# Block-quantised feed-forward weights: nine parts of half size per matrix, one in each projection chunk, and the block scales from a scalar and two tensors

## The chip, the cores and the metric

One core of a Trainium2 chip runs the whole program. The metric is device time in microseconds (us), the median of several executions; lower is better. The engines are TensorE (PE, with PEld for its weight loads), VectorE (DVE), ScalarE (ACT), GpSimd (POOL) and SyncE (SP), which issues the DMAs. Each engine runs its own instructions in the order in which they were written, and waits on semaphores for the others.

## What is computed

The kernel is one pre-norm transformer block over X of shape (8, 2048, 256) in float32:

```
x = x + attention(layernorm(x))     Q = xpos(x Wq), K = xpos(x Wk), V = x Wv
                                    (softmax(Q K^T) * 0.9^|n-m|) V
x = x + ffn(layernorm(x))           down(silu(gate(x)) * up(x)), 704 hidden features

quantised(v), for every block of 16 values along a row, before each linear layer of ffn:
    scale = max(max|v| / 6, 1e-12)
    v / scale rounded to the nearest of 0, .5, 1, 1.5, 2, 3, 4, 6 with its sign, times scale
```

The three feed-forward weights (gate, up, down) are quantised like the activations. Each is held as 128 partitions x 1408 values, so 88 blocks of 16 in a partition.

## The kernel before, in words

**Two stages.** The first stage goes over the input in 32 chunks of 512 rows (batch by batch, four chunks each; the last four chunks are batch 0, which stays on the chip). A chunk is normalised, transposed on TensorE, multiplied with Wk, Wq and Wv, rotated (xpos) and written to DRAM. The second stage goes over 128 row tiles: scores, softmax, decay, values and the feed-forward layers. The change touches the first stage alone.

**A chunk on each engine.** PE does in this order the keys (12 matmuls of 512 columns, tile score), the transposes of the next chunk (L492, 8), queries (12 more) and values (24 of 256). VectorE does, for chunk c: the statistics of chunk c+2 (L1039 to L1047), the rotation of the keys (L1061 to L1063, tile rot_k), the lower half of the next chunk's transposed input (L1052, tile xT), the rotation of the queries (L1061 to L1063, tile rot_q), and then one part of the weights, if any. In the last four chunks it also keeps the values on the chip (L1078, vals) before that part. POOL does: the reciprocal standard deviation of chunk c+2 (L859, rstd), the sum of the rotated keys (L863, rot_k), the sum of the rotated queries (L869, q_stage), the lower half of the keys (L874, keys), and then its own part of the weights, if any. ScalarE normalises chunk c+2 in place (L693, L697, x_in) once rstd is there, and PE transposes that in the middle of the chunk after.

**The weights.** They are quantised in the shade of the first stage by `weights(u)` on VectorE and on POOL, called at the end of each chunk u with `n, part = divmod(u - W_FROM, W_CHUNKS)`: n is the matrix (gate, up, down). With W_CHUNKS = 10, VectorE does for matrix n in chunks 2 + 10n to 7 + 10n: block maxima (L1089), scales and their reciprocals (L1011, L1013), the division by the scales (L1093), the exponent (L1016), the rounding grid (L1019) and the rounding (L1023), each over the whole matrix. POOL does in chunks 8 + 10n to 11 + 10n the subtraction of the grid (L884), in two halves, and the multiplication by the scales (L887), in two halves. The sources and results are slices of buffers that the second stage uses later: gate_in, hq_buf and down_in for the matrices, h_buf for the grid, xv, xe and xq for maxima and scales. SP loads matrix n in chunk n * W_CHUNKS (L379).

A part of VectorE starts when the rotation of the queries is done, at which moment POOL's sum of the queries (L869) has its data as well. The lines that set this:

```
for i in range(B):
    for c in range(NC):
        chunk(i, c)
        weights(i * NC + c)
```

Of the kernel before, what the change touches and what calls it, by code (L numbers as in the profile page):

```python
# [11 lines left out]
ALU = mybir.AluOpType  # L12
# [3 lines left out]
P = 128  # L16
# [31 lines left out]
WARM = (30, 12)  # L48
W_FROM, W_CHUNKS = 2, 10
V_SPLIT = (10, 12, 14, 0, 1, 3, 5, 7)  # L50
# [73 lines left out]
def build(nc, X, WQ, WK, WV, WG, WU, WD, rot_tab, decay_tab, eye, out):  # L124
# [5 lines left out]
    with ExitStack() as ctx:  # L130
# [34 lines left out]
        st2, mv2, var2, rstd2, rstd6 = sb("st2", [P, 6]), sb("mv2", [P, 2]), sb("var2", [P, 1]), sb("rstd2", [P, 1]), sb("rstd6", [P, 1])  # L165
        aggr_pad = sb("aggr_pad", [P, 1])
        minus_half, six, minus_rstd = sb("minus_half", [P, CT]), sb("six", [P, 1]), sb("minus_rstd", [P, CT])
        smax, nmax = sb("smax", [P, 2]), sb("nmax", [P, 2])
# [72 lines left out]
        hq_step, hv_ready, hg_ready, hq_ready = sem("hq_step"), sem("hv_ready"), sem("hg_ready"), sem("hq_ready")  # L241
        NSTEP_W, NSTEP_LN2, NSTEP_XQ, NSTEP_HQ = 6, 2, 6, 5

# [42 lines left out]
        def blocks(ap):  # L286
            return ap.rearrange("p (b k) -> p b k", k=QB)
# [562 lines left out]
        def _(pool):  # L850
# [26 lines left out]
            def weights(u):  # L877

                n, part = divmod(u - W_FROM, W_CHUNKS)
                h, part = part % 2, part // 2  # L880
                half, few = slice(h * WC // 2, (h + 1) * WC // 2), slice(h * WB // 2, (h + 1) * WB // 2)
                if 0 <= n < 3 and part == 3:
                    pool.wait_ge(w_rounded, n + 1)
                    pool.tensor_tensor(w_stage[n][:, half], w_stage[n][:, half], w_exp[:, half], ALU.subtract).then_inc(w_levelled, 1)  # L884
                if 0 <= n < 3 and part == 4:
                    pool.wait_ge(w_levelled, 2 * n + h + 1)
                    pool.tensor_tensor(blocks(w_stage[n][:, half]), blocks(w_stage[n][:, half]), spread(ws[n][:, few], WB // 2), ALU.mult).then_inc(w_quant, 1)  # L887
# [107 lines left out]
        def _(dve):  # L995
# [13 lines left out]
            def scales(then, wait, am, s, rs):  # L1009

                then(dve.tensor_scalar(s, am, SIXTH, 1e-12, ALU.mult, ALU.max))  # L1011
                wait()
                then(dve.reciprocal(rs, s))  # L1013
# [66 lines left out]
            def weights(u):  # L1080

                n, part = divmod(u - W_FROM, W_CHUNKS)
                if not 0 <= n < 3 or part > 5:
                    return
                then, wait, count = chain(w_step, n * NSTEP_W + (0, 1, 3, 4, 5, 6)[part])
                wait()
                if part == 0:
                    dve.wait_ge(w_loaded[n], 16)
                    then(dve.tensor_reduce(wam, blocks(w_stage[n]), AX.X, ALU.max, apply_absolute_value=True))  # L1089
                elif part == 1:  # L1090
                    scales(then, wait, wam, ws[n], wrs)
                elif part == 2:
                    then(dve.tensor_tensor(blocks(w_stage[n]), blocks(w_stage[n]), spread(wrs, WB), ALU.mult))  # L1093
                elif part == 3:
                    if n:
                        dve.wait_ge(w_levelled, 2 * n)
                    exponent(then, w_stage[n], w_exp)
                elif part == 4:
                    grid(then, w_exp)
                else:  # L1100
                    rounded(w_stage[n], w_exp, w_rounded)

# [10 lines left out]
            for x in mv1:  # L1113
                dve.memset(x[:, :, 2], EPS).then_inc(eps_set, 1)
            dve.wait_ge(eps_set, 2)
            def projection_weights(order):
# [236 lines left out]
```

## Time and profile before

| what | us |
|---|---|
| median of 3 runs | 2570.81 (2567.68 to 2571.44) |
| the profiled execution, its own time | 2572.08 |
| its span in the profile | 2570.3 |
| PE busy | 2535.4 (99%) |
| VectorE busy | 2148.3 (84%) |
| POOL busy | 1819.8 (71%) |
| ScalarE busy | 1505.4 (59%) |

The granted TensorE clock is 0.997 of full speed over the span. The profile's page gives busy times and groups; its timeline gives single instructions with start, length, engine, line, operation, output and inputs, and in square brackets the idle time of that engine just before and who ended it. The first stage ends at about 319 us, where the first score of the second stage starts. An instruction's length in the timeline includes the time that it stands on its engine without being able to work.

### The profile page before, as it was taken

The page shows a single profiled execution, that of the slowest core. Times are in us where ns is not written, and L with a number is a line of the kernel's source. Part 1 is how long each engine was busy: PE and PEld are TensorE (multiplying, and loading weights), DVE is VectorE, ACT ScalarE, POOL GpSimd, SP SyncE. Part 2 cuts the span into 40 slices and gives each one's busy share as a digit, 9 for nine tenths or more (in the row PEclk, how much of TensorE's full clock was granted, in tenths as well). Part 3 has the DMA queues.
Part 4 walks back from the last instruction along what each step waited for, and adds up shares of the span by engine and source line. Part 5 has one row for each costly group of instructions (what it writes and reads, how often), then busy time and mean ns, then how long its engine had stood idle before and what let it go on. Part 6 is the DMA issues. An engine that isn't in the chain of part 4 may idle for free.

```text
span 2570.3 us, 51983 instructions
## 1 busy us (share of the span) xinstructions
PE 2535.4 (99%) x16188; PEld 2293.8 (89%) x16188; DVE 2148.3 (84%) x4784; ACT 1505.4 (59%) x2966; POOL 1819.8 (71%) x1919
## 2 busy tenths in 40 slices
PE   9999989999999999999999999999999999999998
PEld 8888879999999999989999899989999999989997
DVE  8999868888888888788888888888888888888886
ACT  5666555566656655656555665566566656565654
POOL 6999947667766767667766766667766776667665
PEclk9999999999999999999999999999999999999999
DMA  8777510113111311131111311131113111221110
GB/s 286 278 282 283 192 55 23 44 34 109 40 46 30 110 42 46 32 106 44 34 42 53 98 32 46 36 108 38 46 32 106 44 42 34 78 74 40 38 38 22
DMA packets 163474, 203.29 MB, mean 79 GB/s; under 512 B 15184, under 2 KB 116752, under 8 KB 163216
## 3 DMA queue, kind: packets, MB, share of 16 engines
q1 hardware_dynamic: 163216, 200.01, 24.0%
q8 instruction: 142, 2.33, 0.4%
q14 instruction: 116, 0.95, 0.1%
HBM read 103.42 MB, written 77.59 MB: 70 GB/s over the span
## 4 chain that ended last, share of the span: by engine, by line
PE 81%; DMA 1%; issue 1%; SPq 1%; DVE 1%; POOL 1%; ACT 1%; DVEq 0%; ACTq 0%; POOLq 0%
PE score L483 26%; PE acc L615 19%; PE ring L483 18%; PE acc L483 8%; PE ring L583 6%; PE ring L635 3%; DMA keys<-k_dram 1%; PE ring L574 1%; PE acc L657 1%; SPq L414 1%; ACT probs L783 0%; POOL h_buf L962 0%; POOL h_buf L956 0%; POOL hq_buf L969 0%; DVE h_buf L1250 0%
## 5 line engine op out<-in xcount | busy, mean ns | idle before, releaser
L483 PE MATMUL score<-keys,q_st 128*128 128x512 f32 x3072 | 761.3, 396 | 7.1 <-ACT probs L783 3.4
L483 PEld LDWEIGHTS score<-keys,q_st 128*128 128x128 f32 x3072 | 559.6, 189 | 117.3 <-issue 3.8
L615 PE MATMUL acc<-vals,pT 128*128 128x256 f32 x3984 | 557.1, 287 | 0.8 <-DVE pT L1154 0.8
L941 POOL TENSOR_TENSOR probs<-probs,decay 128x512 f32<-128x512 f32 (+3 forms) x416 | 446.9, 1087 | 144.4 <-ACT probs L783 144.4
L483 PE MATMUL ring<-w_gu,xqT 128*128 128x512 f32 (+1 forms) x2304 | 509.1, 374 | 0.0
L615 PEld LDWEIGHTS acc<-vals,pT 128*128 128x128 f32 x3984 | 499.2, 189 | 6.1 <-DVE pT L1154 2.0
L483 PEld LDWEIGHTS ring<-w_gu,xqT 128*128 128x128 f32 x2304 | 418.6, 188 | 63.2
L753 ACT ACTIVATE pT<-ring 128x512 fp32r<-128x512 f32 (+3 forms) x432 | 226.9, 535 | 380.2 <-PE ring L583 372.7
L1167 DVE TENSOR_REDUCE smax<-score 128x1 f32<-128x1024 f32 x256 | 312.4, 1220 | 105.7 <-PE score L483 104.8
L1154 DVE TENSOR_TENSOR pT<-ring,pT 128x512 fp32r<-128x512 f32 (+3 forms) x432 | 251.0, 606 | 69.0 <-ACT pT L753 67.9
L947 POOL TENSOR_TENSOR xv<-xv,xe 128x256 f32<-128x256 f32 x128 | 94.4, 738 | 274.0 <-DVE xv L1023 274.0
L753 ACT ACTIVATE xqT<-ring 128x256 fp32r<-128x256 f32 x128 | 49.2, 385 | 401.5 <-PE ring L574 401.5
L783 ACT ACTIVATE probs<-score,nmax 128x1024 f32<-128x1024 f32 x256 | 282.8, 1116 | 0.1
L483 PE MATMUL acc<-w_dn,hT 128*128 128x256 f32 x1920 | 239.3, 277 | 4.6 <-DVE hT L1154 4.6
L483 PEld LDWEIGHTS acc<-w_dn,hT 128*128 128x128 f32 x1920 | 236.0, 188 | 5.3 <-DVE hT L1154 5.3
L936 POOL TENSOR_TENSOR edge_probs<-probs,decay 128x128 f32<-128x128 f32 x144 | 69.0, 479 | 228.8 <-ACT probs L783 228.8
L962 POOL TENSOR_TENSOR h_buf<-h_buf 128x704 f32<-128x704 f32 x128 | 218.8, 1709 | 4.3 <-DVE h_buf L1023 4.3
L1250 DVE TENSOR_TENSOR h_buf<-h_buf,ring 128x256 f32<-128x256 f32 (+1 forms) x384 | 144.2, 376 | 75.7 <-ACT h_buf L809 75.4
L753 ACT ACTIVATE hT<-ring 128x512 fp32r<-128x512 f32 (+1 forms) x256 | 125.0, 490 | 124.9 <-PE ring L635 124.9
L1154 DVE TENSOR_TENSOR hT<-ring,hT 128x512 fp32r<-128x512 f32 (+1 forms) x256 | 141.4, 554 | 66.4 <-ACT hT L753 66.4
L583 PE MATMUL ring<-ident,probs 128*128 128x128 f32 x1328 | 195.2, 273 | 0.0
L483 PE MATMUL score<-xT,w_in 128*128 128x512 f32 x768 | 188.9, 395 | 5.8 <-DVE xT L1052 5.8
(132 smaller groups left out, 4619.9 us busy)
## 6 DMA issues: line engine op xcount, KB each, us to landing
k_dram<-keys SPq DMA_DIRECT2D x56, 512.0 KB, 4.7
keys<-k_dram SPq DMA_DIRECT2D x56, 512.0 KB, 7.5
edge<-vals SPq DMA_DIRECT2D x288, 64.0 KB, 2.1
q_raw<-q_dram SPq DMA_DIRECT2D x129, 128.0 KB, 2.6
x_in<-X SPq DMA_DIRECT2D x32, 512.0 KB, 4.5
q_dram<-q_stage SPq DMA_DIRECT2D x32, 512.0 KB, 5.6
x_res<-X SPq DMA_DIRECT2D x128, 128.0 KB, 2.1
out<-x_res SPq DMA_DIRECT2D x128, 128.0 KB, 1.7
```

The costliest lines, as they stand in the source:

```text
L483: mm = pe.matmul(dst, stat(a, k), mov(m, k), start=i == 0, stop=ends and i == n - 1)
L583: mm = pe.transpose(dst[:, n * P:(n + 1) * P], source, ident[:])
L615: mm = pe.matmul(pv_out, pT[g % 2][:, a, j * P:(j + 1) * P], edge[place][:] if kb in edges else vals[m][:, kb, :], start=i == 0, stop=i == ...
L635: mm = pe.transpose(dst[:, j * P:(j + 1) * P], hq[t % 2][:, k * P:(k + 1) * P], ident[:])
L753: act.activation(dst, src, ACT.Copy).then_inc(hi_done, 1)
L783: act.activation(probs[:, h * 2 * CH:(h + 1) * 2 * CH].rearrange("p (j n) -> p j n", j=2), score[:, 2 * h:2 * h + 2, :], ACT.Exp, bias=nma ...
L941: op = pool.tensor_tensor(probs[:, k0:k1], probs[:, k0:k1], decay[:, off + k0:off + k1], ALU.mult)
L947: pool.tensor_tensor(xv[:], xv[:], xe[:], ALU.subtract).then_inc(x_levelled, 1)
L962: pool.tensor_tensor(hv[t % 2], hv[t % 2], he[t % 2], ALU.subtract).then_inc(h_levelled, 1)
L1154: dve.tensor_tensor(dst, src, hi.bitcast(F32), ALU.subtract).then_inc(freed, 1)
L1167: dve.tensor_reduce(smax[:, h:h + 1], score[:, 2 * h:2 * h + 2, :], AX.XY, ALU.max).then_inc(maxed, 1)
L1250: dve.tensor_tensor(hv[t % 2][:, p0:p0 + w], silu[t % 2][:, p0:p0 + w], bank(at, "gu", t, p)[:, w:2 * w], ALU.mult).then_inc(freed, 1)
```

## The change

W_CHUNKS becomes 9, and a matrix takes nine parts on VectorE, one in each chunk from 2 + 9n to 10 + 9n: maxima of the first half, maxima of the second half, scales and reciprocals (whole), division of each half, exponent (whole), grid (whole), rounding of each half. POOL's four half parts of matrix n stand in chunks 10 + 9n to 13 + 9n. For the down matrix these are chunks 28 to 31 as before, and for gate and up they are two and one chunks later. The semaphore counts follow. The scales are made by `scalar_tensor_tensor`, with a second tensor `tiny` (one column of 1e-12, broadcast over the 88 blocks), instead of `tensor_scalar` with two constants.

```diff
@@ -46,7 +46,7 @@
 XR, LAG, LATER = 8, 5, 3
 W_SLOTS = 3
 WARM = (30, 12)
-W_FROM, W_CHUNKS = 2, 10
+W_FROM, W_CHUNKS = 2, 9
 V_SPLIT = (10, 12, 14, 0, 1, 3, 5, 7)
 V_LOAD = (8, 9, 12, 14, 15, 1, 3, 5)
 LINE, UNIT = 512, 32
@@ -164,6 +164,7 @@
         st1, mv1, var1, rstd1 = sb("st1", [P, CT, 6]), *([sb(f"{n}{i}", w) for i in range(2)] for n, w in (("mv1", [P, CT, 3]), ("var1", [P, CT]), ("rstd1", [P, CT])))
         st2, mv2, var2, rstd2, rstd6 = sb("st2", [P, 6]), sb("mv2", [P, 2]), sb("var2", [P, 1]), sb("rstd2", [P, 1]), sb("rstd6", [P, 1])
         aggr_pad = sb("aggr_pad", [P, 1])
+        tiny = sb("tiny", [P, 1])
         minus_half, six, minus_rstd = sb("minus_half", [P, CT]), sb("six", [P, 1]), sb("minus_rstd", [P, CT])
         smax, nmax = sb("smax", [P, 2]), sb("nmax", [P, 2])
         psum_row = sb("psum_row", [P, 2, 2])
@@ -239,7 +240,7 @@
         xq_step, xg_ready, xq_ready = sem("xq_step"), sem("xg_ready"), sem("xq_ready")
         x_levelled, h_levelled = sem("x_levelled"), sem("h_levelled")
         hq_step, hv_ready, hg_ready, hq_ready = sem("hq_step"), sem("hv_ready"), sem("hg_ready"), sem("hq_ready")
-        NSTEP_W, NSTEP_LN2, NSTEP_XQ, NSTEP_HQ = 6, 2, 6, 5
+        NSTEP_W, NSTEP_LN2, NSTEP_XQ, NSTEP_HQ = 8, 2, 6, 5
 
 
         def later(j):
@@ -876,13 +877,13 @@
 
             def weights(u):
 
-                n, part = divmod(u - W_FROM, W_CHUNKS)
-                h, part = part % 2, part // 2
+                n, part = divmod(u - W_FROM - (W_CHUNKS - 1), W_CHUNKS)
+                h = part % 2
                 half, few = slice(h * WC // 2, (h + 1) * WC // 2), slice(h * WB // 2, (h + 1) * WB // 2)
-                if 0 <= n < 3 and part == 3:
-                    pool.wait_ge(w_rounded, n + 1)
+                if 0 <= n < 3 and part // 2 == 0:
+                    pool.wait_ge(w_rounded, 2 * n + h + 1)
                     pool.tensor_tensor(w_stage[n][:, half], w_stage[n][:, half], w_exp[:, half], ALU.subtract).then_inc(w_levelled, 1)
-                if 0 <= n < 3 and part == 4:
+                if 0 <= n < 3 and part // 2 == 1:
                     pool.wait_ge(w_levelled, 2 * n + h + 1)
                     pool.tensor_tensor(blocks(w_stage[n][:, half]), blocks(w_stage[n][:, half]), spread(ws[n][:, few], WB // 2), ALU.mult).then_inc(w_quant, 1)
 
@@ -1008,7 +1009,7 @@
 
             def scales(then, wait, am, s, rs):
 
-                then(dve.tensor_scalar(s, am, SIXTH, 1e-12, ALU.mult, ALU.max))
+                then(dve.scalar_tensor_tensor(s, am, SIXTH, tiny[:, 0:1].to_broadcast([P, am.shape[1]]), ALU.mult, ALU.max))
                 wait()
                 then(dve.reciprocal(rs, s))
 
@@ -1080,25 +1081,28 @@
             def weights(u):
 
                 n, part = divmod(u - W_FROM, W_CHUNKS)
-                if not 0 <= n < 3 or part > 5:
+                if not 0 <= n < 3:
                     return
-                then, wait, count = chain(w_step, n * NSTEP_W + (0, 1, 3, 4, 5, 6)[part])
+                then, wait, count = chain(w_step, n * NSTEP_W + (0, 1, 2, 4, 5, 6, 7, 8, 8)[part])
+                h = int(part in (1, 4, 8))
+                half, few = slice(h * WC // 2, (h + 1) * WC // 2), slice(h * WB // 2, (h + 1) * WB // 2)
                 wait()
-                if part == 0:
-                    dve.wait_ge(w_loaded[n], 16)
-                    then(dve.tensor_reduce(wam, blocks(w_stage[n]), AX.X, ALU.max, apply_absolute_value=True))
-                elif part == 1:
+                if part < 2:
+                    if part == 0:
+                        dve.wait_ge(w_loaded[n], 16)
+                    then(dve.tensor_reduce(wam[:, few], blocks(w_stage[n][:, half]), AX.X, ALU.max, apply_absolute_value=True))
+                elif part == 2:
                     scales(then, wait, wam, ws[n], wrs)
-                elif part == 2:
-                    then(dve.tensor_tensor(blocks(w_stage[n]), blocks(w_stage[n]), spread(wrs, WB), ALU.mult))
-                elif part == 3:
+                elif part < 5:
+                    then(dve.tensor_tensor(blocks(w_stage[n][:, half]), blocks(w_stage[n][:, half]), spread(wrs[:, few], WB // 2), ALU.mult))
+                elif part == 5:
                     if n:
                         dve.wait_ge(w_levelled, 2 * n)
                     exponent(then, w_stage[n], w_exp)
-                elif part == 4:
+                elif part == 6:
                     grid(then, w_exp)
                 else:
-                    rounded(w_stage[n], w_exp, w_rounded)
+                    rounded(w_stage[n][:, half], w_exp[:, half], w_rounded)
 
             def chunk(i, c):
                 if ahead(i, c, 2):
@@ -1112,7 +1116,8 @@
 
             for x in mv1:
                 dve.memset(x[:, :, 2], EPS).then_inc(eps_set, 1)
-            dve.wait_ge(eps_set, 2)
+            dve.memset(tiny[:], 1e-12).then_inc(eps_set, 1)
+            dve.wait_ge(eps_set, 3)
             def projection_weights(order):
 
                 i = (1, 0, 2)[order]
```

**Order on VectorE around the scales.** Both pieces are VectorE's rows at the end of the chunk in which the scales of the up matrix are made (chunk 13 in both programs). rot_q is the rotation of the queries, xq and xe take scales and reciprocals, xv holds the maxima. Before:

```order
L1061 TENSOR_TENSOR rot_q<-score,tab 128x1024
L1062 SCALAR_TENSOR_TENSOR rot_q<-score,tab 128x512
L1063 TENSOR_TENSOR rot_q<-score,tab 128x512
L1011 TENSOR_SCALAR xq<-xv 128x88
L1013 RECIPROCAL xe<-xq 128x88
L1039 BN_STATS st<-x_in 128x6 x4
```

Changed:

```order
L1062 TENSOR_TENSOR rot_q<-score,tab 128x1024
L1063 SCALAR_TENSOR_TENSOR rot_q<-score,tab 128x512
L1064 TENSOR_TENSOR rot_q<-score,tab 128x512
L1012 SCALAR_TENSOR_TENSOR xq<-xv,tiny 128x88
L1014 RECIPROCAL xe<-xq 128x88
L1040 BN_STATS st<-x_in 128x6 x4
```

The place in the chunk and the chunk are the same; the operation reads one tensor more.

**Order on POOL in the same chunk 13.** q_stage is the sum of the queries, keys the lower half of the keys, gate_in the gate matrix. Before:

```order
L859 TENSOR_TENSOR rstd<-var,minus_half 128x4
L863 TENSOR_TENSOR rot_k<-rot_k 128x1024
L869 TENSOR_TENSOR q_stage<-rot_q 128x1024
L874 TENSOR_TENSOR keys<-rot_k,keys 128x2x512
L859 TENSOR_TENSOR rstd<-var,minus_half 128x4
```

Changed:

```order
L860 TENSOR_TENSOR rstd<-var,minus_half 128x4
L864 TENSOR_TENSOR rot_k<-rot_k 128x1024
L870 TENSOR_TENSOR q_stage<-rot_q 128x1024
L875 TENSOR_TENSOR keys<-rot_k,keys 128x2x512
L888 TENSOR_TENSOR gate_in<-gate_in,xq 128x704
L860 TENSOR_TENSOR rstd<-var,minus_half 128x4
```

The last half part of the gate matrix now stands at the end of this chunk; it stood at the end of chunk 11.

**Order on VectorE at the end of chunk 28**, the first of the last four, where the values are kept (vals). Before:

```order
L1063 TENSOR_TENSOR rot_q<-score,tab 128x512
L1078 SCALAR_TENSOR_TENSOR vals<-ring,vals 128x512
L1078 SCALAR_TENSOR_TENSOR vals<-acc,vals 128x512
L1039 BN_STATS st<-x_in 128x6 x4
L1043 MEMSET aggr_pad 128x1
```

Changed:

```order
L1064 TENSOR_TENSOR rot_q<-score,tab 128x512
L1079 SCALAR_TENSOR_TENSOR vals<-ring,vals 128x512
L1079 SCALAR_TENSOR_TENSOR vals<-acc,vals 128x512
L1024 SCALAR_TENSOR_TENSOR down_in<-down_in,h_buf 128x704
L1040 BN_STATS st<-x_in 128x6 x4
L1044 MEMSET aggr_pad 128x1
```

The rounding of the down matrix's second half comes into this chunk, ahead of the statistics of chunk 30; the whole rounding stood in chunk 27.

## Rows read from the trace of the kernel before

**Rows 1.** The page: busy us, share and instructions of each engine.

```profile
PE 2535.4 (99%) x16188; PEld 2293.8 (89%) x16188; DVE 2148.3 (84%) x4784; ACT 1505.4 (59%) x2966; POOL 1819.8 (71%) x1919
```

**Rows 2.** Timeline, PE (start, length, engine, line, output<-input, count, idle before), first stage.

```profile
91.83 1.03 PE L492 MATMUL ring<-ident,x_in 128*128 128x128 f32 x8
...
100.99 1.04 PE L492 MATMUL ring<-ident,x_in 128*128 128x128 f32 x8
...
147.97 1.03 PE L492 MATMUL ring<-ident,x_in 128*128 128x128 f32 x8
...
156.65 3.03 PE L483 MATMUL score<-xT,w_in 128*128 128x512 f32 x12 [2.07 <-DVE xT L1052]
159.51 1.04 PE L492 MATMUL ring<-ident,x_in 128*128 128x128 f32 x8
...
169.59 1.09 PE L492 MATMUL ring<-ident,x_in 128*128 128x128 f32 x8 [0.56 <-ACT x_in L697]
```

**Rows 3.** Timeline, VectorE and POOL, end of chunk 13.

```profile
143.19 2.46 POOL L863 TENSOR_TENSOR rot_k<-rot_k 128x1024 f32<-128x1024 f32 x1
...
145.06 5.36 DVE L1011 TENSOR_SCALAR xq<-xv 128x88 f32<-128x88 f32 x1
...
145.56 2.45 POOL L869 TENSOR_TENSOR q_stage<-rot_q 128x1024 f32<-128x1024 f32 x1
...
147.93 2.43 POOL L874 TENSOR_TENSOR keys<-rot_k,keys 128x1024 fp32r<-128x1024 f32 x1
...
150.45 0.70 DVE L1013 RECIPROCAL xe<-xq 128x88 f32<-128x88 f32 x1
```

**Rows 4.** Line L1011, gate and up: ns min/median/max, first and last start.

```profile
L1011 DVE TENSOR_SCALAR xq<-xv x2: 197/2778/5358, 54.1 to 145.1; 128x88 f32<-128x88 f32 x2
```

**Rows 5.** Line L1238, second stage: ns min/median/max, first and last start.

```profile
L1238 DVE SCALAR_TENSOR_TENSOR xv<-xv,rstd,xrs x128: 470/1084/1302, 353.5 to 2541.5; 128x256 f32<-128x256 f32 x128
```

**Rows 6.** Timeline, VectorE and POOL, second stage, one of the L1238.

```profile
688.57 1.03 POOL L941 TENSOR_TENSOR probs<-probs,decay 128x384 f32<-128x384 f32 x1
688.66 1.22 DVE L1238 SCALAR_TENSOR_TENSOR xv<-xv,rstd,xrs 128x256 f32<-128x256 f32 x1
...
689.54 1.48 POOL L916 TENSOR_TENSOR vals<-v_raw,vals 128x512 fp32r<-128x512 f32 x1
```

**Rows 7.** Timeline, VectorE and POOL, ends of chunks 26 and 27.

```profile
273.05 0.98 DVE L1019 TENSOR_SCALAR h_buf<-h_buf 128x1408 f32<-128x1408 f32 x1
...
281.77 1.74 DVE L1023 SCALAR_TENSOR_TENSOR down_in<-down_in,h_buf 128x1408 f32<-128x1408 f32 x1
282.00 3.77 POOL L869 TENSOR_TENSOR q_stage<-rot_q 128x1024 f32<-128x1024 f32 x1
```

**Rows 8.** Line L1023 at half of a matrix's width, in the second stage.

```profile
L1023 DVE SCALAR_TENSOR_TENSOR h_buf<-h_buf x128: 891/893/1864, 375.5 to 2558.4; 128x704 f32<-128x704 f32 x128
```

**Rows 9.** Timeline, POOL's weight parts of the gate matrix and after.

```profile
113.66 1.73 POOL L884 TENSOR_TENSOR gate_in<-gate_in,h_buf 128x704 f32<-128x704 f32 x1
...
115.33 1.02 POOL L859 TENSOR_TENSOR rstd<-var,minus_half 128x4 f32<-128x4 f32 x1
...
119.90 1.09 PE L492 MATMUL ring<-ident,x_in 128*128 128x128 f32 x8 [0.36 <-ACT x_in L697]
...
135.12 2.45 POOL L863 TENSOR_TENSOR rot_k<-rot_k 128x1024 f32<-128x1024 f32 x1
...
135.66 1.61 DVE L1089 TENSOR_REDUCE xv<-hq_buf 128x88 f32<-128x1408 f32 x1
```

**Rows 10.** Timeline, end of the first stage, chunks 28 and 29.

```profile
293.84 2.40 POOL L874 TENSOR_TENSOR keys<-rot_k,keys 128x1024 fp32r<-128x1024 f32 x1
...
295.26 1.40 DVE L1039 BATCH_NORM_STATS2 st<-x_in 128x6 f32<-128x256 f32 x4
...
300.89 3.04 PE L483 MATMUL score<-xT,w_in 128*128 128x512 f32 x12 [0.96 <-DVE xT L1052]
...
303.30 2.40 POOL L869 TENSOR_TENSOR q_stage<-rot_q 128x1024 f32<-128x1024 f32 x1 [1.20 <-DVE rot_q L1063]
```

## The prediction

> **What bounds the kernel now.** The page comes first: PE is busy 99% of the span, VectorE 84%, POOL 71% [rows 1]. So only time in which PE stands still, or runs behind its own pace, can be won. The change touches the first stage alone, so the next view is PE's timeline there. The transposes in the middle of a chunk are a good mark. Undisturbed they come every 9.16 us (91.83 to 100.99) [rows 2]; that is PE's own pace, and no engine beside it can better it. Around the scales of the up matrix the marks are 11.54 us apart (147.97 to 159.51), then 10.08 us (to 169.59) [rows 2]: 2.38 and 0.92 us over the pace, 3.3 us together. The first part of it ends when VectorE delivers xT, the second when ScalarE has normalised x_in, which hangs on POOL and through it on VectorE [rows 2]. The down matrix has the same pattern, so there are two such places; the gate matrix has none.
>
> **Where those 3.3 us come from.** VectorE's and POOL's timeline of chunk 13 shows it [rows 3]. The scales' tensor_scalar, 88 columns, stands on VectorE for 5.36 us, from 145.06 to 150.42. The same instruction takes 197 ns for the gate matrix [rows 4], so about 5.16 us of it are waiting. POOL ran three additions without a gap meanwhile, the last of them until 150.36, and the tensor_scalar ends 0.06 us after it [rows 3]. I read this as a resource that both need, and at which the tensor_scalar is passed over at two change-overs (L863 to L869, L869 to L874). For gate POOL stood idle, so it took 0.2 us.
>
> How much may VectorE lose before PE notices? Without a part a chunk costs it 7.7 us (274.03 to 281.77) [rows 7], against PE's 9.16, so about 1.4 us are free in each. The wait and PE's stall give the stock on top: 5.16 of wait, some 0.9 of own work (0.2 and the reciprocal's 0.70 [rows 3]), less 1.4, less the 2.4 us stall, leaves 2.3 us. A delay of up to about 3.7 us in one chunk is free.
>
> **The change, part by part.**
>
> 1. *The new form of the scales.* What does a scalar_tensor_tensor with both tensors in SBUF do beside a busy POOL? L1238 is one: 470 ns at best, 1084 ns in the middle, 1302 ns at worst over 128 executions [rows 5]. So it waits too. One piece shows how: it starts 0.09 us into a POOL addition of 1.03 us, ends 0.3 us after it, and POOL's next instruction, which had been dispatched at once, is the one that gets longer (1.48 us) [rows 6]. It waits for the one POOL instruction that is running, and gets in at the next change-over. The Trainium skill ("SBUF — State Buffer", section "Who interferes with whom") speaks against the change here: it says that a VectorE instruction with two SBUF inputs contends with a GpSimd instruction that reads SBUF, just as the two-port modes that a tensor_scalar may take. This trace agrees that both wait, but the two differ in how many change-overs they lose, which the page does not tell.
>
> 2. *How long it waits.* For up and down, POOL's last half part of the matrix before now stands in the same chunk as the scales, with three other halves in the three chunks before. So POOL is late there. The nearest row: one chunk after POOL's last half part, its L863 ends at 137.57, and VectorE is done with the queries at 135.66 [rows 9]: 1.9 us late. I take 1.9 us of wait; ends are 0 and a whole L863, 2.4 us. With 0.2 us and the reciprocal it makes 2.8 us in that chunk, under the 3.7 us. The two chunks that follow hold half divisions with two SBUF inputs, which wait about 1 and 0.2 us; each half costs 0.9 us [rows 8], less 1.4 free, so the lag stays under the stock. PE does not stand still: **-3.3 us twice, -6.6 us**.
>
> 3. *Halves instead of wholes.* A whole rounding costs VectorE 1.74 us and prolongs POOL's addition beside it to 3.77 us instead of 2.4 [rows 7, 3]. Chunks with a whole part exceed PE's pace (7.7 + 1.7 = 9.4 us), chunks with a half do not (8.6). That frees POOL up to 0.7 us per half part (half of 3.77 less 2.4); what of it reaches PE I put at -0.3 us in all, an estimate between 0 and -0.7. A half costs 0.89 us [rows 8], so the fixed part of each split is under 0.1 us, hidden in VectorE's free 1.4 us.
>
> 4. *POOL's halves, moved by two and one chunks.* Each makes POOL's chunk longer than PE's: from 113.66 it needs 1.73 us, and the next rstd starts at 115.33 [rows 9]; four in a row use up POOL's stock, and PE's mark at 119.90 waits 0.36 us for x_in [rows 9]. After the change the four halves find POOL less late from earlier whole parts, but now there are half roundings and the scales in the same chunks. I take 0, with ends of -0.5 and +1.5 us for each matrix.
>
> 5. *The last half rounding, new in chunk 28.* Here nothing hides it. In the last four chunks VectorE waits for the values, and then goes straight to the statistics of chunk 30 at 295.26; PE waits 0.96 us for xT at 300.89; POOL waits 1.20 us for the queries at 303.30 and has no gap until the second stage starts [rows 10]. So what delays VectorE at 295.26 delays the end. The half rounding has two SBUF inputs and meets POOL's L874, 293.84 to 296.24 [rows 10]. The half rounding in chunk 27 is 0.85 us shorter than the whole one (1.74 less 0.89), which lets everything come about 0.8 us earlier; then it waits for L874 (which comes earlier as well) and takes 0.89 us. Statistics at about 296.1 instead of 295.26: **+0.85 us**. The ends are 0 (all absorbed) and +1.7 us (nothing gained in chunk 27).
>
> 6. *The rest.* One memset and a longer wait before the first statistics, while the first input is still on its way: 0. The loads of up and down come one and two chunks earlier, still well before they are read: 0. The order on PE, ScalarE and SP is the same but for those two loads.
>
> Sum: -6.6 - 0.3 + 0 + 0.85 = about **-6.0 us**. The profiled execution took 2572.08 us, so 2566.1 on its terms. The median of the runs shown is 1.3 us lower, 2570.81, so **2564.8 us**, -0.23%. What a measurement of this kernel can tell from no change is about 0.2%, 5.1 us; the forecast lies just beyond that. With the ends of items 3 to 5 its own range is 2562.5 to 2567.5.
>
> **The rivals.**
>
> *A. POOL's queue takes part of it back.* In chunks 10 to 13, and 19 to 22, POOL's halves and VectorE's halves stand together and hold each other up. For it: POOL's stock is used up there already [rows 9], and every VectorE instruction with two SBUF inputs takes its length from POOL [rows 7]. Against: the parts in chunks 11 and 12 are reductions of one input. At the upper ends of items 4 and 5 (+1.5 twice, +1.7), without item 3: -6.6 + 3.0 + 1.7 = -1.9 us, 2568.9 us. Chance 0.20.
>
> *B. The wait moves to the exponent.* L1016 and L1019 stay tensor_scalar instructions with two constants. They stand in chunks 16, 17, 25 and 26. If POOL is still half a microsecond late there, as at 145 us, they are passed over as L1011 was. VectorE then already carries over a microsecond of lag from the scales, so each costs PE about 4.0 us instead of 3.3. -6.6 + 8.0 - 0.3 + 0.85 = +2.0, 2572.8 us: no change. Against: after each division POOL and VectorE leave the shared resource together, and VectorE's next part comes within 0.2 us of the end of L863, as with L1019 and L1023 before, which got in (they took 0.98 and 1.74 us, and L869 was dispatched 0.23 us after L1023) [rows 7]. Chance 0.07.
>
> *C. Slower: the new form is passed over as well.* Decides: whether the new instruction gets in at the first change-over. If not, it waits for L863's rest (1.9), L869 (2.4), L874 (2.4) and now POOL's half part too, which used to stand two chunks or one chunk earlier (1.4 to 1.7 [rows 9]): 8.1 us against 5.16 now. Each microsecond more goes through to PE, so +3.0 us at two places, less 0.6 for the cheaper maxima before. +6.0 - 0.6 - 0.3 + 0.85 = +5.95 us, 2576.8 us. The same section of the Trainium skill calls the shared pair an exclusive lock that blocks the other fully, for any such instruction; by that rule the new form has no advantage. Against it stand 128 executions of L1238 with at most 1302 ns [rows 5] beside POOL instructions of 1.0 us and more. Chance 0.07.
>
> **How the numbers follow.** The forecast has 0.66, A 0.20, B 0.07, C 0.07. The time is the forecast's, 2564.8 us. The range goes from 2562.0 to 2570.0: from the forecast's lower end, with half a microsecond for the scatter of the runs, over A; it leaves out B and C. Faster by over 0.2% means under 2565.7: four fifths of the forecast, 0.53. Slower by over 0.2%: C and a little of B, 0.08. Within 0.2%: the rest, 0.39.
>
> **What would show it.** In the changed profile the scales of up and down (now L1012) take 0.2 to 2.6 us, not over 5; POOL's L870 after them is at most 0.3 us longer. PE's marks in chunks 14 to 16 and 23 to 25 stay within 0.5 us of 9.16 us. VectorE's statistics after the half rounding of chunk 28 come later behind the values than before, and PE's wait for xT at that point is about 1.8 us. The second stage has the same length. If L1012 is over 5 us, C holds; if L1017 or L1020 is, B holds; if waits of PE for x_in grow in chunks 11 to 14, A.

## The result and the profile after

| | before | changed |
|---|---|---|
| median us, 20 executions each on one chip | 2571.46 (2561.26 to 2575.76) | 2579.32 (2567.92 to 2582.80) |
| the profiled execution, its own time | 2572.08 | 2579.47 |
| its span | 2570.3 | 2575.2 |
| first score of the second stage starts at | 318.92 | 325.32 |
| own time less span | 1.8 | 4.3 |

The changed kernel is slower: ratio 1.0026, 95% interval [1.0018, 1.0034]; 7.9 us on the medians. The forecast of 2564.8 us had the wrong sign. The two profiled executions, 7.4 us apart, put it in three places: the first stage is 6.4 us longer, 2.5 us lie outside the span, and the second stage is 1.5 us shorter, which means nothing: its program is the same, and in the fourteen profiles of this document it takes 2249.1 to 2255.2 us. One of the seven executions of e2 below was slow (10464 us) and is left out of its ratio.

The page shows nothing of this; against [rows 1] the busy times hardly move.

```profile
PE 2536.5 (98%) x16188; PEld 2297.4 (89%) x16188; DVE 2152.2 (84%) x4794; ACT 1505.8 (58%) x2966; POOL 1816.3 (71%) x1919
```

The scales (now L1012) show it at once, beside [rows 4]: 243 ns for gate, and 8.08 and 8.09 us for up and down, where the tensor_scalar stood 5.36 and 5.35 us.

```profile
L1012 DVE SCALAR_TENSOR_TENSOR xq<-xv,tiny x2: 243/4162/8082, 62.8 to 143.9; 128x88 f32<-128x88 f32 x2
L1012 DVE SCALAR_TENSOR_TENSOR xv<-xv,tiny x1: 8092/8092/8092, 234.0 to 234.0; 128x88 f32<-128x88 f32 x1
```

The timeline of VectorE and POOL, end of chunk 13, beside [rows 3]:

```profile
143.48 2.39 POOL L864 TENSOR_TENSOR rot_k<-rot_k 128x1024 f32<-128x1024 f32 x1
...
143.95 8.08 DVE L1012 SCALAR_TENSOR_TENSOR xq<-xv,tiny 128x88 f32<-128x88 f32 x1
...
145.84 2.38 POOL L870 TENSOR_TENSOR q_stage<-rot_q 128x1024 f32<-128x1024 f32 x1
...
148.18 2.39 POOL L875 TENSOR_TENSOR keys<-rot_k,keys 128x1024 fp32r<-128x1024 f32 x1
...
150.53 1.39 POOL L888 TENSOR_TENSOR gate_in<-gate_in,xq 128x704 f32<-128x704 f32 x1
...
152.06 0.70 DVE L1014 RECIPROCAL xe<-xq 128x88 f32<-128x88 f32 x1
...
154.72 1.01 POOL L860 TENSOR_TENSOR rstd<-var,minus_half 128x4 f32<-128x4 f32 x1 [2.80 <-DVE var L1048]
```

POOL runs four instructions without a gap, and none is longer than it is alone. The new form asks 0.47 us into the first and ends 0.11 us after the last: it is passed over at three change-overs. (A change-over is the moment at which POOL ends one instruction and begins the next.) Before, the last half part (now L888) wasn't in this chunk, and there were two. Of the 2.72 us by which the wait grew, L888 is about 1.35, and the rest of L864, of which 1.92 us were still to run instead of 0.59, is about 1.33. POOL stops after L888 only because its next instruction, L860, needs VectorE's statistics, which stand behind the waiting instruction.

PE's timeline, beside [rows 2]:

```profile
147.04 1.09 PE L493 MATMUL ring<-ident,x_in 128*128 128x128 f32 x8
...
158.26 5.15 PE L484 MATMUL score<-xT,w_in 128*128 128x512 f32 x12 [4.54 <-DVE xT L1053]
163.25 1.03 PE L493 MATMUL ring<-ident,x_in 128*128 128x128 f32 x8
```

The mark takes 16.21 us to come instead of 9.16, 7.05 too many; at the down matrix it is 15.63, 6.47 too many. Before, each place cost 3.3 over two intervals. PE waits 4.54 us, and the 12 matmuls behind the wait then take 5.15 us instead of 3.0. The windows of that stretch say why (columns: us, busy time of PE, PEld, DVE, ACT and POOL with the number of instructions, granted clock as a share of full speed, DMA share, GB/s):

```profile
140.00:153.00 13.00, 12.97 (x83) 11.42 (x82) 12.71 (x10) 6.75 (x14) 11.92 (x7) 1.00 0.81 275
153.00:158.00 5.00, 0.71 (x7) 0.51 (x5) 4.92 (x15) 2.21 (x6) 1.92 (x2) 0.81 0.86 336
158.00:163.00 5.00, 4.74 (x11) 3.76 (x12) 4.96 (x14) 3.23 (x7) 3.78 (x2) 0.51 0.12 48
163.00:170.00 7.00, 7.00 (x48) 6.37 (x47) 6.68 (x11) 4.12 (x10) 6.57 (x5) 1.00 0.74 249
```

While PE had nothing to do the granted clock fell to its lower level, 1.2 GHz, and stayed there for the first 5 us of work: 2.1 us that the prediction had nowhere (1.5 at the down matrix, where the 12 matmuls take 4.57 us). The end of the stage, beside [rows 10]:

```profile
298.25 2.38 POOL L875 TENSOR_TENSOR keys<-rot_k,keys 128x1024 fp32r<-128x1024 f32 x1
...
299.10 2.28 DVE L1024 SCALAR_TENSOR_TENSOR down_in<-down_in,h_buf 128x704 f32<-128x704 f32 x1
...
300.60 2.35 POOL L885 TENSOR_TENSOR down_in<-down_in,h_buf 128x704 f32<-128x704 f32 x1
...
301.30 1.40 DVE L1040 BATCH_NORM_STATS2 st<-x_in 128x6 f32<-128x256 f32 x4
...
307.28 3.06 PE L484 MATMUL score<-xT,w_in 128*128 128x512 f32 x12 [2.11 <-DVE xT L1053]
```

Here VectorE does get in at the first change-over, after 1.4 us, and POOL's L885 beside it is lengthened instead. PE's wait for xT is 2.11 us against 0.96 before.

**Ledger of the first stage.** Scales of up and down: 13.5 us over PE's pace against about 6.6, +6.9. The last mark (298.58 to 310.18): 11.60 us against 10.48, +1.1. All else, where halves stand in place of wholes and POOL's halves are moved: +6.4 less those two, -1.6.

### The profile page after: what moved, and what is told of

The parts are those of the page before. It is cut to its first block, busy times and chain, and to the rows that moved or that the text cites. A ratio compares the mean times of both kernels' runs of the same rounds, so it can differ in the third digit from the quotient of the medians.

```text
span 2575.2 us, 51993 instructions
## 1 busy us (share of the span) xinstructions
PE 2536.5 (98%) x16188; PEld 2297.4 (89%) x16188; DVE 2152.2 (84%) x4794; ACT 1505.8 (58%) x2966; POOL 1816.3 (71%) x1919
## 4 chain that ended last, share of the span: by engine, by line
PE 83%; POOL 1%; DVE 0%; issue 0%; DMA 0%; ACT 0%; SPq 0%; POOLq 0%; DVEq 0%; ACTq 0%
PE score L484 26%; PE acc L616 19%; PE ring L484 18%; PE acc L484 8%; PE ring L584 6%; PE ring L636 3%; PE acc L658 1%; PE ring L575 1%; DMA keys<-k_dram 0%; SPq L415 0%; POOL h_buf L963 0%; ACT probs L784 0%; POOL h_buf L957 0%; POOL hq_buf L970 0%; POOL probs L942 0%
```

## The experiments

The theory after the result: a VectorE instruction that needs what POOL holds is not sure of the next change-over; behind back-to-back POOL instructions it may stand until POOL runs dry. Rivals: the new form, the width of the instruction, or the nine parts themselves. Every ratio below is to the kernel before, and where a cut of code leaves lines out, three dots mark it.

**e1, the form alone.** On the kernel before, only the form (and the tile `tiny` with its memset):

```diff
-then(dve.tensor_scalar(s, am, SIXTH, 1e-12, ALU.mult, ALU.max))
+then(dve.scalar_tensor_tensor(s, am, SIXTH, tiny[:, 0:1].to_broadcast([P, am.shape[1]]), ALU.mult, ALU.max))
```

> The kernel before, with only the scales made by a scalar and two tensors. Theory 1 (the form makes no difference: in this place both forms are passed over at every change-over while POOL has a ready instruction): the scales of up and down take 5.3 to 5.4 us as before, the time is that of before within 2 us. Theory 2 (the two-tensor form waits for one POOL instruction only): they take under 1.2 us and the kernel is about 6.5 us faster than before.

Measured: 2573.18 us against 2571.96, ratio 1.000 [0.999, 1.0009].

```profile
L1012 DVE SCALAR_TENSOR_TENSOR xq<-xv,tiny x2: 241/2817/5393, 53.6 to 144.6; 128x88 f32<-128x88 f32 x2
L1012 DVE SCALAR_TENSOR_TENSOR xv<-xv,tiny x1: 5383/5383/5383, 240.7 to 240.7; 128x88 f32<-128x88 f32 x1
```

5.39 and 5.38 us where the old form took 5.36 and 5.35. The form changes nothing about the wait.

**e2, the parts alone.** The changed kernel with the old form (the same two lines, the other way round).

> The changed kernel with the scales made by the old form, a tensor and two constants. Theory 1 (the loss comes from POOL's last half part, which now stands behind its three additions in the chunk of the scales): the scales take 8.0 to 8.2 us for up and down, the time is that of the changed kernel, 7 to 8 us over before. Theory 2 (the new form is what costs): back to 5.4 us and to the time of before.

Measured: 2579.75 us (median of all seven), 1.003 [1.0018, 1.0043]. The nine parts alone are the loss. The profiled execution was the fastest of them, 2574.44 us, and shows both outcomes: 8.05 us for up, but only 1.99 us for down:

```profile
233.71 2.39 POOL L864 TENSOR_TENSOR rot_k<-rot_k 128x1024 f32<-128x1024 f32 x1
...
234.19 1.99 DVE L1012 TENSOR_SCALAR xv<-xv 128x88 f32<-128x88 f32 x1
236.06 2.40 POOL L870 TENSOR_TENSOR q_stage<-rot_q 128x1024 f32<-128x1024 f32 x1
```

It asks 0.48 us into L864, almost as up did here (0.46) and in the changed kernel (0.47), yet it gets in. PE does not stall there; the marks are 9.41 and 9.23 us apart. So where in the POOL instruction the request falls does not fix the outcome by itself.

**e3, scales on ScalarE.** The changed kernel; ScalarE multiplies the maxima by a sixth, VectorE keeps the reciprocal (the lower bound 1e-12 is left out).

```diff
-scales(then, wait, wam, ws[n], wrs)
+dve.wait_ge(w_scaled, n + 1)
...
+then(dve.reciprocal(wrs, ws[n]))
...
+act.wait_ge(w_step, n * NSTEP_W + 2)
+act.activation(ws[n], wam, ACT.Copy, scale=SIXTH).then_inc(w_scaled, 1)
```

> The changed kernel with the scales made on ScalarE early in the chunk, and only the reciprocal on VectorE; the lower bound of 1e-12 of a scale is left out. Theory 1 (the wait of the scales is the whole loss, with the slower TensorE clock that follows it): no VectorE instruction over 3 us beside the weights, PE's marks within 0.6 us of 9.16, about 13.5 us less than the changed kernel and 5 to 6 us less than before. Rival (what POOL's queue lacks it lacks anyway; the half parts take the place of the wait): within 3 us of before.

Measured: 2576.36 us, 1.0019 [1.0009, 1.0029]: 3.0 us under the changed kernel, where the first theory asked for 13.5. The wait moves to the half division one chunk later, a tensor_tensor with two SBUF inputs:

```profile
152.38 2.42 POOL L871 TENSOR_TENSOR rot_k<-rot_k 128x1024 f32<-128x1024 f32 x1
152.89 7.36 DVE L1109 TENSOR_TENSOR hq_buf<-hq_buf,xe 128x704 f32<-128x704 f32 x1
...
154.75 2.40 POOL L877 TENSOR_TENSOR q_stage<-rot_q 128x1024 f32<-128x1024 f32 x1
...
157.10 2.40 POOL L882 TENSOR_TENSOR keys<-rot_k,keys 128x1024 fp32r<-128x1024 f32 x1
```

The marks there are 15.12 us apart, and 12.70 at the down matrix, where the half division stands 7.38 us.

**e4, width.** e3 with a probe at the scales' old place: a scalar_tensor_tensor with two SBUF inputs, 704 columns for up and 256 for down, result unused.

```diff
+w = (0, 704, 256)[n]
...
+dve.scalar_tensor_tensor(spare[:, 0:w], spare[:, 0:w], 1.0, spare[:, 704:704 + w], ALU.mult, ALU.max)
```

> The same with ScalarE's scales, and in the place of the old scales one VectorE instruction more with two SBUF inputs, on spare data: 704 columns for up, 256 for down (work that nothing needs). Theory place (whatever its width, an instruction that needs what POOL holds is passed over there until POOL runs dry): 704 takes 8.5 to 9 us, 256 takes 8.1 to 8.5 us. Theory width (only the short one of 88 columns is passed over): 704 takes 0.9 to 2.9 us, 256 0.4 to 2.4 us.

Measured: one execution, 2579.19 us, and

```profile
L1094 DVE SCALAR_TENSOR_TENSOR h_buf<-h_buf x2: 8275/8503/8731, 143.6 to 233.8; 128x704 f32<-128x704 f32 x1, 128x256 f32<-128x256 f32 x1
```

8.73 and 8.28 us, with marks of 16.45 and 15.51 us as in the changed kernel. 88, 256 and 704 columns wait alike. So neither form nor width decides; what is left is the place, that is, what POOL has ready when VectorE asks.

**e5, the same step in the kernel before.** As e3, but with ten chunks and whole parts (lower bound left out as well).

> The kernel before with whole parts, but the scales made on ScalarE early in the chunk and only the reciprocal on VectorE; the lower bound of 1e-12 of a scale is left out. The first VectorE instruction that needs what POOL holds now comes one chunk later, in chunks 14 and 24, three chunks after POOL's last half part. Theory 1 (what counts is whether POOL has a ready instruction behind the running one when VectorE asks; by the trace of before POOL is 0.5 us late in chunk 13 and so not late in chunk 14): no wait over 0.5 us at the division, PE's marks within 0.6 us of 9.16 up to chunk 28, 6 to 7 us faster than before. Rival (the wait only moves to the next such instruction, as in the nine-part kernel with ScalarE's scales): 4.9 us of wait at the division and no gain, within 1.5 us of before.

Measured: 2563.37 us against 2571.95, 0.997 [0.9959, 0.9982]. From 27 us on no interval between marks is more than 0.31 us over 9.16 but the last (9.78 us), and the first stage ends at 309.81. The two waits are worth at least the 6.6 us that the prediction put on them (8.6 by the medians), and here nothing takes their place. When the division of up asks, at 153.11 us, POOL stands idle: its L876 waits 0.74 us for VectorE's queries and starts at 153.33. In e3 POOL was 0.51 us into L871 at that moment and had more behind it. In this kernel POOL has no weight part in the chunk before a division; in e3 it has one, which is how I read the difference.

**e6 and e7, a gap everywhere.** POOL waits for its own previous instruction before L870, L875 and its weight parts; e6 in the changed kernel, e7 in the kernel before.

```diff
+pool.wait_ge(rot_added, 2 * g + 1)
 pool.tensor_tensor(q_stage[c % 2][:], rot_q[:, 0:2, :], rot_q[:, 2:4, :], ALU.add).then_inc(rot_added, 1)
...
+pool.wait_ge(rot_added, 2 * (i * NC + c) + 2)
 pool.tensor_tensor(keys[1][:, :, cols], rot_k[c % 2][:, 0:2, :], keys[0][:, :, cols].bitcast(F32),
...
+pool.wait_ge(k_split, i * NC + c + 1 + PRIME)
 weights(i * NC + c)
```

> The changed kernel, in which POOL waits, ahead of its sum of the queries, its lower half of the keys and its weight parts, until its own instruction before has ended, so that it is not back to back with it. Theory 1 (VectorE is passed over because POOL's next instruction is taken up before the running one has let go; a gap lets VectorE in): the scales of up and down take 1.5 to 2.4 us instead of 8.1, the kernel is 11 to 14 us faster than the changed one and 4 to 6 us faster than before. Rival (POOL has precedence whenever it has an instruction that is ready, gap or not): 8 to 9 us each, and the kernel as slow as the changed one or slower by up to 2 us.

> The same gaps on POOL in the kernel before, with its old form of the scales. Theory 1: the old form gets in at the first change-over as well: 0.5 to 1 us instead of 5.36, 6 to 7 us faster than before. Rival: 5.4 to 5.8 us, and the time of before or up to 1 us more.

Measured: e6 2575.22 us, 1.0016 [1.0006, 1.0026]; e7 2573.56 us, 1.0008 [0.9999, 1.0018]. In e7 the old form gets in at the first change-over:

```profile
147.35 2.41 POOL L863 TENSOR_TENSOR rot_k<-rot_k 128x1024 f32<-128x1024 f32 x1
...
148.65 1.17 DVE L1014 TENSOR_SCALAR xq<-xv 128x88 f32<-128x88 f32 x1
149.93 2.41 POOL L870 TENSOR_TENSOR q_stage<-rot_q 128x1024 f32<-128x1024 f32 x1 [0.17 <-POOL rot_k L863]
```

The long waits are gone, but e6 gets back only 4.1 us of what the changed kernel lost, where 11 to 14 were expected, and e7 nothing, where 6 to 7 were: around POOL's weight parts the marks are now 9.8 to 10.3 us apart in either kernel, with PE waiting up to 0.87 us for x_in. I read it as POOL having no time for three or four gaps in a full chunk.

**e8, both half roundings of down in chunk 27.** It takes the new rounding out of chunk 28.

```diff
+elif part == 7:
+    for x in range(2):
+        half = slice(x * WC // 2, (x + 1) * WC // 2)
+        rounded(w_stage[n][:, half], w_exp[:, half], w_rounded)
```

> The changed kernel, with the two half roundings of the down matrix both in chunk 27 and none in chunk 28. Theory 1 (the half rounding in chunk 28 has nothing to hide it and costs its length and its wait for POOL): PE's wait for xT in chunk 29 falls from 2.1 to about 1.0 us and the first stage ends 1.1 us earlier; the two waits of 8.1 us stay. Rival (it is absorbed, and the end is set elsewhere): no change at the end of the first stage. The sum of both is too small to be told from the times; the mark is read in the trace.

Measured: 2579.78 us, 1.0033 [1.0024, 1.0043]. PE's wait for xT falls from 2.11 to 0.24 us, but a wait of 0.57 us for x_in comes up and the one for q_st grows from 0.24 to 0.59 us, and from the mark at 290 us to the end of the stage it takes 35.41 us against 35.94 (289.38 to 325.32). Half a microsecond of the 1.1 comes back, and at this scatter no time shows it.

**e9 and e10, one gap.** The wait before L870 only, in the chunks of the scales of up and down: e9 the changed kernel, e10 the kernel before (`(1, 1), (2, 1)`).

```diff
+if divmod(g - W_FROM, W_CHUNKS) in ((1, 2), (2, 2)):
+    pool.wait_ge(rot_added, 2 * g + 1)
 pool.tensor_tensor(q_stage[c % 2][:], rot_q[:, 0:2, :], rot_q[:, 2:4, :], ALU.add).then_inc(rot_added, 1)
```

> The changed kernel; in chunks 13 and 22 alone POOL waits for its own sum of the keys before it starts the sum of the queries, a gap of about 0.17 us at the first change-over. If the forecast was right in all but the change-over at which the new form gets in, the scales wait some 2 us, PE's marks in chunks 13 to 15 and 22 to 24 stay within 0.5 us of 9.16, the two stalls of 7.05 and 6.47 us go, and the time is about 2579.3 - 13 = 2566 us. If whichever instruction with two SBUF inputs comes first is passed over as long as POOL is late, the scales get in, but the half division in the next chunk takes 5 to 7 us, as with the scales on ScalarE, and the time is about 2575 us.

> The kernel before; the same single gap in chunks 13 and 23. If the gap is enough and costs no more than its 0.17 us, the scales take about 1.2 us instead of 5.36, the two stalls (3.3 us each place) go, and the time is 6 us under the kernel before, about 2566 us. If gaps cost POOL time that it does not have there (as all of them together did), a wait of PE for x_in takes the place and the time is within 2 us of the kernel before.

Measured: e9 2568.85 us, e10 2565.11 us, against 2572.05 of before; 0.999 [0.998, 0.9999] and 0.997 [0.9957, 0.9982]. e9 is 10.5 us under the changed kernel for 0.34 us of gaps:

```profile
143.63 2.41 POOL L864 TENSOR_TENSOR rot_k<-rot_k 128x1024 f32<-128x1024 f32 x1
...
144.10 2.06 DVE L1014 SCALAR_TENSOR_TENSOR xq<-xv,tiny 128x88 f32<-128x88 f32 x1
...
146.22 2.40 POOL L872 TENSOR_TENSOR q_stage<-rot_q 128x1024 f32<-128x1024 f32 x1 [0.17 <-POOL rot_k L864]
...
154.57 1.84 DVE L1099 TENSOR_TENSOR hq_buf<-hq_buf,xe 128x704 f32<-128x704 f32 x1
155.63 3.04 POOL L872 TENSOR_TENSOR q_stage<-rot_q 128x1024 f32<-128x1024 f32 x1
```

This is the forecast's picture: 2.06 us for the scales, L872 right behind, marks of 9.64 and 9.25 us in the two chunks after. The half division in the next chunk, the place that stood 7.36 us in e3, gets in after 1 us although POOL leaves it no gap. So the second expectation did not come true. In e10 the scales take 0.66 us instead of 5.36, and the marks in the two chunks after each place are 9.16 to 9.19 us apart:

```profile
144.79 0.66 DVE L1013 TENSOR_SCALAR xq<-xv 128x88 f32<-128x88 f32 x1
...
145.56 2.42 POOL L871 TENSOR_TENSOR q_stage<-rot_q 128x1024 f32<-128x1024 f32 x1 [0.17 <-POOL rot_k L863]
```

e10 is the fastest version that computes everything.

**e11, the lower bound kept.** e5 with ScalarE writing beside a column of 1e-12, and VectorE taking the larger by a reduction of one input.

```diff
-then(dve.reciprocal(wrs, ws[n]))
+then(dve.tensor_reduce(ws[n], pair[:], AX.X, ALU.max))
+wait()
+then(dve.reciprocal(wrs, ws[n]))
```

> The kernel before with the scaling of the maxima by a sixth on ScalarE, and the lower bound 1e-12 kept: ScalarE writes beside a column of 1e-12, and VectorE takes the larger of the two by a tensor_reduce with one input, then the reciprocal. If a VectorE instruction with one input is never passed over, the reduction takes under 0.4 us, the marks are as in the version without the lower bound (within 0.5 us of 9.16), and the time is about 2564 us. If it was the short program part alone that helped there, the reduction is passed over in chunks 13 and 23 and takes 5 us, and the time is about 2572 us.

Measured: 2569.96 us, 0.9987 [0.9977, 0.9996]. The reduction runs in the midst of L871, and does not wait:

```profile
143.28 2.40 POOL L871 TENSOR_TENSOR rot_k<-rot_k 128x1024 f32<-128x1024 f32 x1
...
145.18 0.33 DVE L1100 TENSOR_REDUCE xq<-pair 128x88 f32<-128x176 f32 x1
```

The time is 6 us above the expected 2564: 2.7 of them lie outside the span (4.5 against 1.8), the rest inside it (2565.4 against 2561.5 in e5, medians). In the profiled executions the first stage has 1.9 of it (311.67 against 309.81); the rest I can't place.

**e12, three idle instructions at the start.** The changed kernel, for the time outside the span.

```diff
+pool.memset(spare[:, 2:3], 1.0).then_inc(constants_set, 1)
...
+for k in range(2):
+    dve.memset(spare[:, k:k + 1], 1.0).then_inc(eps_set, 1)
```

> The changed kernel with three instructions more at the very start that do nothing for the result (one memset on POOL, two on VectorE). It asks only for the time that lies outside the span: 4.3 us in the changed kernel against 1.8 before. If that depends on where the last instructions lie in the program, it falls to about 2 us here and the time to about 2577 us; if it belongs to the nine parts themselves, it stays at 4.0 us or more and the time at about 2579.5 us. The span is the same as in the changed kernel in both cases.

Measured: 2578.18 us, 1.0016 [1.0005, 1.0027]. The time outside the span has a median of 1.84 us in ten executions; in the changed kernel it was 4.26 in twenty. The time itself falls by only 1.1 us, for these ten spans have a median 1.3 us longer, which is within their scatter. The long waits stay (marks 16.34 and 15.67 us).

| version | median us | first stage ends | own time less span, median |
|---|---|---|---|
| before | 2571.5 to 2572.1 | 318.92 | 1.8 to 2.0 |
| changed | 2579.32 | 325.32 | 4.3 |
| e9, changed and one gap | 2568.85 | 313.00 | 4.1 |
| e10, before and one gap | 2565.11 | 310.61 | 1.9 |
| e5, before, scales on ScalarE, no lower bound | 2563.37 | 309.81 | 1.8 |

## Why the prediction was wrong

**What bounds the kernel: right.** PE's marks at 9.16 us, the two places, and the wait as their cause: e5 and e10 take the waits away and gain 6.9 to 8.6 us, where 6.6 were on offer.

**Item 1 failed**, in the sentence "It waits for the one POOL instruction that is running, and gets in at the next change-over". What the runs showed in its place: the instruction is passed over at three change-overs and stands 8.08 and 8.09 us, where 0.2 to 2.6 were forecast, and PE loses 7.05 and 6.47 us there instead of nothing. That makes +6.9 us where -6.6 were forecast, 13.5 of the 14.5 us by which the forecast missed. The step was argued from L1238 in the second stage [rows 5, 6]. Those rows are right for their place, but they were carried over as a property of the instruction. e1 shows that the form has no share in it, e4 that the width has none. [rows 3] showed this very place losing two change-overs, and place was the nearer evidence. The Trainium skill ("SBUF — State Buffer", section "Who interferes with whom") treats the two forms alike; here the measurements agree, 5.39 us for the one and 5.36 us for the other. The prediction had cited it, and weighed it at 0.07.

**Item 2, the size, was nearly right for what it assumed.** With the gap of e9 the scales take 2.06 us (forecast 1.9 and 0.2), and the first stage ends at 313.00 instead of 318.92: -5.9 us, where the items sum to -6.0. That agreement is in part luck. PE does lose something: the marks at each place are 0.57 us over the pace together, so the two places are worth -5.4 us and not -6.6, and the -1.6 us of the next paragraph make up for it (-5.4 - 1.6 + 1.1 for the last mark).

**Item 3 (-0.3) and item 4 (0): better than forecast,** -1.6 us together, in the changed kernel and in e9 alike. In the changed kernel PE no longer waits for x_in in the chunks of POOL's halves, which I put down to there being no whole roundings before them (not tried alone). A half takes 882 ns where it waits for nothing (forecast 0.89 us).

**Item 5: right mechanism, 0.25 us short.** VectorE got in at the change-over, as assumed; the last mark is 1.1 us later against +0.85. The miss is in the sum: L874's end at 296.24, 0.8 us earlier, and 0.89 us more make 296.3 and not 296.1, so +1.1. e8 takes the rounding away and gets 0.5 us of it back; then PE waits for POOL's results instead.

**Item 6: a term was missing.** The 2.5 us outside the span belong to no step of the change. e12 takes it away with three idle instructions, and e11, with ten chunks, has it (4.5 us). So it does not belong to the nine parts as such; what in a program sets it stays open. Without it the changed kernel is still 5 us slower by its span (medians 2575.1 and 2570.0).

**The range.** The upper ends of items 3 to 5 sum to -1.9 us, 2568.9 us, as rival A has it; the 2567.5 us given for the forecast's own range does not follow from them.

**Rival C is what happened.** It named place, length and reason: 8.1 us forecast, 8.08 and 8.09 measured. Its price was short: 3.0 us at each place, 3.75 and 3.2 measured (7.05 and 6.47 less 3.3), since PE comes back at the lower clock. The stall itself grew by only 2.47 us (4.54 for 2.07). Rivals A and B did not happen: in chunks 11 to 14 there is no PE wait for x_in, and L1017 and L1020 take 0.88 to 1.0 us.

**What stays open** is who wins a change-over. At the scales of up and down (in e3 the half divisions, in e4 the probes), in the profiles of before, changed, e1 to e4, e8 and e12, 15 requests lost all of theirs and one (e2, down) won its first. In chunk 28 of the changed kernel and in the half divisions of e9 they won too, with POOL just as gapless. And in the kernel before the exponents, grids and roundings, which asked in the last 0.3 us of L863, all nine won. The place and the gap matter, and how many instructions POOL has lined up sets how long a loser waits; the moment of the request has a part in it but does not decide alone (0.47 us in, lost; 0.48 us in, won). The spans of the changed kernel reach over 15 us (2563.8 to 2578.7) and those of e9 over 5 (2563.1 to 2568.4), as if the executions of the changed kernel lost sometimes and won at other times. Only one of them has a profile, so that reading is argued and not shown.

## What to carry to other kernels

When VectorE shares a resource with a busy POOL, don't count the instruction's duration; count how many instructions POOL has ready behind the running one, for the wait can be all of them (2.0, 5.4 or 8.1 us here for a fifth of a microsecond of work). Adding work to POOL behind such a place lengthens VectorE's wait, even if the work itself is hidden. Two cures worked here: one single gap in POOL's queue at that place (e10, -6.9 us for 0.34), or moving the work to something that did not wait, ScalarE and a reduction of one input (e5, -8.6 us without the lower bound; e11, with it, -2.1 us, because 2.7 us came back outside the span and some inside). One input alone is no cure: the tensor_scalar with its two constants has only one and stood 5.36 us. Gaps everywhere give it all back (e7).

## What was unexpected of the hardware

- A wait of POOL on its own previous instruction opens a gap of 0.17 us between two POOL instructions, and a VectorE instruction that lost two or three change-overs without it gets in (e10: 0.66 us instead of 5.36; e9: 2.06 instead of 8.08).
- PE's clock after a stall: after 4.54 us of idleness the granted clock was 0.51 over 5 us. After 2.10 us it fell too in e1, but not after 2.07 us in the kernel before (3.03 us for the 12 matmuls, [rows 2]), nor after 3.16 us in the second place of e3. Within e3 alone the 12 matmuls took 5.49 us after 3.15 us of idleness, 3.02 after 3.16, and 4.60 after 2.24. Two windows:

```profile
157.00:161.00 4.00, 4.00 (x15) 3.18 (x14) 4.00 (x8) 2.17 (x4) 2.78 (x2) 0.61 0.17 70
```

```profile
255.00:259.00 4.00, 3.85 (x21) 3.30 (x22) 4.00 (x8) 3.49 (x7) 2.79 (x2) 1.00 0.07 29
```

The first is e1's, 12 matmuls in 4.61 us; the second e3's, 12 in 3.02 us. So a stall of PE costs its length, or its length and 1.5 to 2.5 us more, and the length alone doesn't tell which.

- The time outside the span has a median of 1.8 to 2.0 us in some versions and of 4.1 to 4.5 in others: three idle instructions moved it by 2.4 us.
